# Cross-attention in four layers: products P·V of successive key tiles issued together, 14 probability buffers instead of 6

## The reference

```python
q = hidden_states @ Wq            # and k, v from encoder_hidden_states
logits = jnp.einsum('bhqd,bhkd->bhqk', q, k) * scale
logits = logits + col_bias[None, None, :, :]
probs = jax.nn.softmax(logits, axis=-1)
out = jnp.einsum('bhqk,bhkd->bhqd', probs, v)
out = out @ Wo + bo
out = out + residual
```

## Time and profile before

| what | us |
|---|---|
| median of three runs | 5466.34 |
| lowest and highest run | 5460.77, 5468.5 |
| span of the profiled execution | 5460.9 |
| TensorE busy with matmuls | 5173.7 (95%) |
| VectorE busy | 3684.8 (67%) |
| GpSimd busy | 2695.0 (49%) |
| ScalarE busy | 2245.5 (41%) |

### The profile page before, as it was taken

How to read it: one execution, slowest core, us unless ns; L and a number is a source line. 1 busy time by engine, 2 the same in 40 slices (tenths; PEclk the granted TensorE clock), 3 DMA queues, 4 the chain that set the end, 5 groups by cost and what they waited for, 6 DMA issues and landing times.

```text
span 5460.9 us, 81559 instructions
## 1 busy us (share of the span) xinstructions
PE 5173.7 (95%) x21484; PEld 2708.9 (50%) x21484; DVE 3684.8 (67%) x5908; ACT 2245.5 (41%) x4042; POOL 2695.0 (49%) x2048
## 2 busy tenths in 40 slices
PE   7999999999979898987999999999989999999999
PEld 4455545554444444444455555555445455545554
DVE  6767676767667676765767666676676667676767
ACT  2433344334425455552444444344424444444443
POOL 1656565656510101011656566666625656565655
PEclk8999999999979999997999999999989999999999
DMA  2010101010020101001010101010011010101010
GB/s 72 14 27 14 27 14 27 14 27 14 14 43 15 24 16 23 16 15 26 14 26 13 26 13 26 13 26 19 8 28 24 16 26 13 26 13 26 13 26 17
DMA packets 40356, 116.57 MB, mean 21 GB/s; under 512 B 7350, under 2 KB 20150, under 8 KB 35068
## 3 DMA queue, kind: packets, MB, share of 16 engines
q1 hardware_dynamic: 39938, 112.04, 9.4%
HBM read 26.86 MB, written 2.10 MB: 5 GB/s over the span
## 4 chain that ended last, share of the span: by engine, by line
PE 82%; issue 7%; DVE 6%; DMA 2%; SPq 1%; ACT 0%; DVEq 0%; POOL 0%; ACTq 0%; POOLq 0%
PE OB L654 19%; PE SS L594 13%; PE ST L625 11%; PE ST L627 9%; PE ST L551 5%; PE ST L567 4%; PE OB L786 4%; DVE mpart L1087 4%; PE ST L765 3%; PE SS L744 3%; PE ST L572 3%; PE ST L672 3%; PE ZB L607 2%; DMA Q<-rawQ 1%; PE ZB L744 1%
## 5 line engine op out<-in xcount | busy, mean ns | idle before, releaser
L282 POOL TENSOR_TENSOR acc<-acc,P 128x512 f32<-128x512 f32 (+1 forms) x1776 | 2362.5, 1356 | 455.1 <-ACT P L934 308.8
L934 ACT ACTIVATE P<-ST 128x512 f32<-128x512 f32 (+1 forms) x2496 | 1385.5, 597 | 2012.0 <-PE ST L627 1703.7
L1087 DVE TENSOR_REDUCE mpart<-SS 128x1 f32<-128x400 f32 (+1 forms) x3072 | 1665.0, 563 | 764.1 <-PE SS L594 709.1
L654 PE MATMUL OB<-P,V 128*64 128x512 f32 (+1 forms) x4992 | 1348.0, 618 | 1.1
L594 PE MATMUL SS<-KS,Q 128*128 128x400 f32 (+1 forms) x3072 | 1171.6, 387 | 70.2 <-DVE mpart L1087 67.1
L625 PE MATMUL ST<-Q,K 128*128 128x512 f32 (+1 forms) x2496 | 1061.3, 425 | 32.9 <-issue 18.3
L594 PEld LDWEIGHTS SS<-KS,Q 128*128 128x128 f32 x3072 | 585.0, 192 | 860.0 <-DVE mpart L1087 758.5
L627 PE MATMUL ST<-Q,K 128*128 128x512 f32 (+1 forms) x2496 | 989.6, 396 | 0.0
L278 POOL TENSOR_TENSOR acc<-P 128x512 f32<-128x512 f32 x192 | 241.3, 1278 | 1410.8 <-ACT P L934 1310.8
L625 PEld LDWEIGHTS ST<-Q,K 128*128 128x128 f32 (+1 forms) x2496 | 462.8, 185 | 515.8 <-ACT P L934 348.3
L1106 DVE RECIPROCAL R<-ZB 128x64 f32<-128x64 f32 (+1 forms) x432 | 371.3, 860 | 408.9 <-PE ZB L607 408.9
(11 more groups left out here) (126 smaller groups left out, 3608.1 us busy)
## 6 DMA issues: line engine op xcount, KB each, us to landing
Q<-Q SPq DMA_DIRECT2D x48, 512.0 KB, 4.5
KS<-K SPq DMA_DIRECT2D x48, 400.5 KB, 3.8
K<-K SPq DMA_DIRECT2D x48, 400.5 KB, 5.3
Q<-Q SPq DMA_DIRECT2D x32, 256.0 KB, 4.3
wk<-in_wk SPq DMA_DIRECT2D x25, 256.0 KB, 4.4
wv<-in_wv SPq DMA_DIRECT2D x25, 256.0 KB, 4.6
Q<-rawQ SPq DMA_DIRECT2D x16, 256.0 KB, 3.8
wq<-in_wq SPq DMA_DIRECT2D x25, 128.0 KB, 4.3
```

What stands on the lines that cost most here:

```text
L282: eng.tensor_tensor(out, out, P[0:rows_of(t), u % NP, :], ALU.add).then_inc(done, raised)
L654: last = pe.matmul(OB[64 * jj:64 * jj + 64, :], V[0:k, t, 64 * b:64 * b + 64], P[0:k, (2 * s + jj) % NP, :], start=t == 0, stop=t == KT - 1)
L934: act.activation(P[0:k, u % NP, :], ST[u % 4][0:k, :], ACT.Exp, scale=SCALE).then_inc(act_p, 1)
L1087: dve.tensor_reduce(mpart[:, i // len(KCH), i % len(KCH):i % len(KCH) + 1], SS[i % 2][:, 0:w], AX.X, ALU.max).then_inc(dve_s, 1)
```

## The change

`P` has 14 buffers of 128x512 instead of 6. The product groups of two successive steps (of three at steps 10 to 12 and 23 to 25) are issued together, after the score pairs of the last of them. All max tiles of a step now stand before the product group. Layer 1 and the loads keep to the first six buffers. ScalarE's, VectorE's and GpSimd's programs change only in the number of buffers.

```diff
-NP = 6
+NP = 14
+RUNS = (2, 2, 2, 2, 2, 3) * 2
+RUN_END = [sum(RUNS[:i + 1]) - 1 for i in range(len(RUNS))]
...
+                def weigh(r):
+                    t = r % KT
+                    k = rows_of(t)
+                    for jj in range(2):
+                        last = pe.matmul(OB[64 * jj:64 * jj + 64, :], V[0:k, t, 64 * b:64 * b + 64],
+                                         P[0:k, (2 * r + jj) % NP, :], start=t == 0, stop=t == KT - 1)
+                    last.then_inc(pe_pv, 1)
...
                     for jj in range(2):
                         if s + 1 < STEPS:
                             scores(s + 1, jj)
                         tiles = s_next(tiles)
-                    pr.wait(act_p, 2 * UNITS, g * UNITS + 2 * s + 2)
-                    if t == 0:
-                        pr.wait(act_o, 4, 2 * g + c2)
-                    for jj in range(2):
-                        last = pe.matmul(OB[64 * jj:64 * jj + 64, :], V[0:k, t, 64 * b:64 * b + 64],
-                                         P[0:k, (2 * s + jj) % NP, :], start=t == 0, stop=t == KT - 1)
-                    last.then_inc(pe_pv, 1)
-                    s_next(tiles, last=True)
+                    tiles = s_next(tiles) if s in RUN_END else s_next(tiles, last=True)
+                    if s in RUN_END:
+                        first = s + 1 - RUNS[RUN_END.index(s)]
+                        if first % KT == 0:
+                            pr.wait(act_o, 4, 2 * g + c2)
+                        pr.wait(act_p, 2 * UNITS, g * UNITS + 2 * s + 2)
+                        for r in range(first, s + 1):
+                            weigh(r)
+                        s_next(tiles, last=True)
```

More of the change, by code:

```diff
@@ L179, in attention_layers @@
         gwo = rawK[:, (2 * CCT + CT) * 128:(2 * CCT + CT) * 128 + C]
-        K4hi = P[:, :, :].rearrange("p n q -> p (n q)")[:, 0:KP].bitcast(F32R)
+        K4hi = P[:, 0:6, :].rearrange("p n q -> p (n q)")[:, 0:KP].bitcast(F32R)
         K4lo = acc[:, :, :, :].rearrange("p a b q -> p (a b q)")[:, 0:KP].bitcast(F32R)
         Q4hi, Q4lo = Q2[0], rawQ[:, :].bitcast(F32R)
-        PG = [P[:, i, :] for i in range(NP)] + [acc[:, i // 2, i % 2, :] for i in range(3)]
+        PG = [P[:, i, :] for i in range(6)] + [acc[:, i // 2, i % 2, :] for i in range(3)]
         Z = acc[:, 1, 1, :]
@@ L304, in _ @@
                              .rearrange("(t p) c -> p t c", p=128)).then_inc(d_x, 16)
-            sp.dma_start(P[:, :, :], a["ctx"][0:768, :].rearrange("(t p) c -> p t c", p=128)).then_inc(d_in, 16)
+            sp.dma_start(P[:, 0:6, :], a["ctx"][0:768, :].rearrange("(t p) c -> p t c", p=128)).then_inc(d_in, 16)
             sp.dma_start(acc[:, :, :, :].rearrange("p a b c -> p (a b) c"),
@@ L642, in attend @@
                     c2, t = s // KT, s % KT
-                    k = rows_of(t)
                     tiles = [] if other is None else list(s_units(s))
```

## The result

The changed kernel takes 5720.6 us (median of 4 runs, 5717.66 to 5722.25), against 5463.9 us for the kernel before, timed again on the same chip: ratio 1.0467, interval 1.0454 to 1.048. It is slower by 257 us; the forecast had +166. The time lies inside the range of 5440 to 5750, just above the likeliest case of 5540 to 5720. The direction and the mechanism held, and one of the four terms was too small.

The account below looks back on a forecast made before the run. TensorE was taken as the bound, busy 95% of the span. Per attend -5.25 + 4.93 + 4.86 - 0.55 = +3.99 us, times 45, less 14, gave +166: 5632 us expected, range 5440 to 5750.

Parts of the forecast that it names:

- Term 1: TensorE's merged product groups: fewer changes of layout, 0.35 us saved per merged group, 5.25 us per attend with max tiles.
- The rival of uncovered weight loads: In merged groups the second group's weights don't load under the first: +66 us on the forecast, 5698; chance 0.06.
- Terms 2 and 4: Third max tile right behind the second waits: 4.93 us lost per attend; half the old reduce waits end: -0.55.
- Term 3: VectorE's `lo_part`, add and reciprocal between two steps of a run delay TensorE's max tiles: 4.86 us lost per attend.
- This spares steps 4|5 and 8|9: With only two tiles in the run's second step, VectorE's other work between the steps there costs nothing.
- I take the means: VectorE's `lo_part` and add priced at mean durations, 1.054 or 1.006 and 1.132 us, as GpSimd is busy four fifths.
- The upper end given for the term: VectorE's work inside runs at 1.61 us per `lo_part` and 1.30 per add: 6.7 us per attend.
- Costed at nothing: Waits for ScalarE's exponentials, GpSimd's lag in adds under 14 buffers, and the larger `P`: no cost.
- VectorE keeps up: Rival: VectorE's slack covers all new waits of max tiles, so the merging gain remains: 5167 us, or 5216; chance 0.06.
- Only term 2 bites: Rival: only max tiles two in a row cost; VectorE's extra work hides under the products: 5413 us; chance 0.10.
- The clock falls: Rival: new waits bring one attend in ten to the lower clock, some 50 us longer each: +240, 5870; chance 0.04.
- What would show it: Expected signs: x8 groups of 1.9 to 2.0 us, max tile waits of 350 to 450 us, attends of about 73 us.

Follow-up runs that it names:

- the last short-reduce pair: Merged kernel with VectorE's other work behind the run's reduces, 64-column reduces, 65-row adds given to GpSimd: 5158.7 us; against the unmerged kernel with equally short reduces: 5344.0 us.
- run 17: Not a follow-up kernel: steps 17 and 18 of an attend, whose product groups the changed kernel issues together, unlike the kernel before; its fifth max tile waits 1.65 us.
- the kernel with other work last: The changed kernel with VectorE's low parts, adds, reciprocals and divisions of a run put behind all its reduces: 5491.2 us, ratio 1.0045.
- the kernel with short reduces: The changed kernel with VectorE's reduces of the wide layers reading 64 columns of each max tile instead of 400: 5333.1 us, ratio 0.976.
- the kernel with work moved and reduces short: The changed kernel with VectorE's other work behind the reduces of its run and reduces of 64 columns instead of 400: 5477.7 us, ratio 1.002.

## Why the prediction was right in direction and short in size

- **Term 1, -250 us: held.** The group of two is 1.87 us and that of three 2.73 us, to the hundredth as worked out, and the last short-reduce pair shows some 245 us. The rival of uncovered weight loads is refuted by the same rows: by it the second step of a group would cost 0.96 instead of 0.86 us. So the rule of the Trainium skill that was weighed against the row does not describe these groups.
- **Terms 2 and 4, +197 us: held.** The pair of tiles costs 0.65 instead of 0.36 us, and the kernel that has this part of the change alone costs 208 us.
- **Term 3, +219 us: too small, and the step that failed.** The rest of the measured sum is 257 + 250 - 208 = 299 us, 80 more than forecast. About 16 of the 80 are the clock (below), which no term of the sum held; some 64 are the waits themselves. 231 us came back when VectorE's other work left the inside of the runs, most of the clock's part with it. The remaining 68 are mostly waits that a kernel with that work behind the reduces has as well, such as the one of 1.13 us behind two `lo_part`; how they divide stays open. Two sentences of the step were wrong. "This spares steps 4|5 and 8|9" looked only inside the run: VectorE's delay goes through the product group of 1.87 us and reaches the third tile of the next run (0.82 us at 910.10). And "I take the means" was wrong for adds inside a run: the one shown in run 17|18 took 1.46 us where 1.13 was assumed, because it met an add of GpSimd. The upper end given for the term, +82 us, comes close, but it counted longer instructions only and not the waits passed on.
- **Costed at nothing: held.** Product groups wait 2.5 us for exponentials in all, and 14 buffers alone change nothing.
- **Rivals.** That VectorE keeps up was right for neither part. "Only term 2 bites", with VectorE's extra work in the run's last step, was put at 5413 us; the kernel that does just this took 5491, in part because a product group is too short for what it must hide (3.17 us under 1.87). "The clock falls" came true in a small way, at 16 us instead of 240; its rows stand behind this list.
- **What would show it.** Waits were forecast at 350 to 450 us and are 337; a short wait hides up to 0.17 us of itself under the matmul before it, so this count is no measure of the loss. The attend was forecast at about 73 us and took 76.5, of which 1.6 are the lower clock. At full clock the two kinds of attend lose 6.0 and 5.6 us, where 4.0 was forecast. GpSimd is busy 55 of 76 us in the longer attend (73%), where the step on the means had four fifths in either kernel.

The clock. Eight of the 17 attends with a stretch at the lower clock have it at their start, where the kernel before has its stretches too. In the nine others it follows the long waits of term 3, as here behind the waits of runs 17|18 and 21|22:

```profile
4469.89 0.45 PE L596 MATMUL SS<-KS,Q 128*128 128x400 f32 x1 [1.65 <-DVE mpart L1097]
...
4482.59 0.45 PE L596 MATMUL SS<-KS,Q 128*128 128x402 f32 x1 [1.74 <-DVE mpart L1097]
4482.97 3.46 PE L636 MATMUL OB<-P,V 128*64 128x512 f32 x8
```

and the stretch behind the second wait:

```profile
4483.50:4486.50 3.00, 3.00 (x9) 0.62 (x5) 0.62 (x2) 0.00 (x0) 2.00 (x2) 0.50 0.00 0
```

The product group there takes 3.46 us instead of 1.94. In the kernel with other work last, where such long waits are gone, nine attends have a stretch at the lower clock, all at their start.

## What to carry to other kernels

Merging groups of matmuls saves the changes between them, but also takes away the regular pauses in which a neighbouring engine caught up. So list what that engine does between two steps and how long its loop with TensorE is (here 1.02 us over two banks), follow a delay until the neighbour's queue is really empty, not only to the end of the merged run, and price its instructions by those that run beside the third engine, not by the mean. If such a group is merged, the neighbour's other work has to move to where the pause now is, and must fit into it. And long waits have a second price: look at the granted clock of single attends, since the mean of the run hides it.

## What was not expected of the hardware

VectorE's add of two SBUF operands takes 0.69 us alone. Beside adds of GpSimd it ended, in each of three traces, 0.55 us after the GpSimd add that it had waited for. In run 17|18 of the changed kernel that one ended at 944.06 and VectorE's at 944.61 (1.46 us in all). In the kernel with short reduces it ended at 949.48 and VectorE's, begun at 948.33, at 950.03:

```profile
948.20 1.28 POOL L284 TENSOR_TENSOR acc<-acc,P 128x512 f32<-128x512 f32 x1 [2.08 <-ACT P L944]
```

And in the kernel with work moved and reduces short, three in a row ended at 3058.89 and VectorE's at 3059.44 (5.33 us). These rows read as if the add did not share the memory with GpSimd's, but waited and then ran. The Trainium skill (SBUF — State Buffer, SBUF: two separate sides) describes the port that the two engines share as an exclusive lock that the first one keeps for its whole instruction; these rows agree.

How many of GpSimd's adds it waits for is not always the same. In the kernel before, the `lo_part` at 860.03 stood beside six adds of GpSimd without a pause and still took only 1.69 us, so it came in between two of them. In the kernel with work moved and reduces short, six adds lasted until 3055.24 and three more until 3058.89, and the add of 65 rows, begun at 3054.11, was passed over three times:

```profile
858.45 8.46 POOL L282 TENSOR_TENSOR acc<-acc,P 128x512 f32<-128x512 f32 x6 [1.43 <-DVE acc L282]
```

```profile
3046.43 8.81 POOL L284 TENSOR_TENSOR acc<-acc,P 128x512 f32<-128x512 f32 x6 [1.42 <-DVE acc L284]
```

Why the one comes in and the other does not, no run shows. That it happened in all 45 attends of the kernel with short reduces, and in none of the kernel with the same order and full reduces, says that a shorter neighbour can bring the engines into such a meeting.

TensorE's wait of 4.25 us was followed by a stretch at granted clock 0.50, and so were, in nine attends of the changed kernel, waits of 1.6 to 1.7 us in its runs. In other attends, waits of the same length were followed by none: the one of 4608.16 to 4683.99 has granted clock 1.00 throughout.
